# Linear attention and a mixture of experts on one core: key values turned by VectorE and a way over DRAM, in place of TensorE transposes

## The reference

```
xn  = layernorm(x)                                  # rows of 128
# linear attention, H = 16 heads of DK = 8, F = 64 features a head
q, k, v = xn @ Wq + bq, xn @ Wk + bk, xn @ Wv + bv   # split into heads
qp = relu(q @ rw) + EPS;  kp = relu(k @ rw) + EPS    # per head: 8 -> 64
kv   = sum over the 256 rows of kp^T v               # per batch and head, 64 x 8
out  = (qp @ kv) / (qp @ kp.sum(rows) + EPS);  attn = out @ Wo + bo
# experts, E = 8, 128 -> 512 -> 128, one expert a row
gate = p1 / (p1 + p2) of softmax(xn @ wr + br);  e = argmax
ffn  = gate * (gelu(xn @ w1[e] + b1[e]) @ w2[e] + b2[e])
result = x + attn + ffn
```

## Time and profile before

| what | value |
|---|---|
| profiled execution | 205.19 us, its span 203.2 us |
| median of 3 runs | 205.25 us (204.72 to 205.96) |
| PE busy | 189.6 us, 93% |
| DVE, ACT, POOL busy | 66%, 65%, 60% |
| granted TensorE clock, mean | 0.988 |
| DMA | 29.48 MB, 145 GB/s over the span |

### The profile page before, as it was taken

One profiled execution on the slowest core, in us unless ns is written; L12 is line 12 of the kernel. 1 busy time (PEld: TensorE's weight loads), 2 busy tenths in 40 slices (PEclk: granted clock), 3 DMA queues, 4 the chain that ended last, 5 costly groups with the idle time before them and its releaser, 6 DMA issues. The chain is left out here.

```text
span 203.2 us, 6913 instructions
## 1 busy us (share of the span) xinstructions
PE 189.6 (93%) x2353; PEld 151.1 (74%) x2353; DVE 134.9 (66%) x467; ACT 133.0 (65%) x319; POOL 121.0 (60%) x156
## 2 busy tenths in 40 slices
PE   6799999898899999999999999999999999999960
PEld 6557676565566666666666668999999999999950
DVE  5899697668888877777777786555555545545540
ACT  3268868659977777777777754755655655655620
POOL 2059793101137666666666210788888888888884
PEclk9999999999999999999999999999999999999995
DMA  4730599999912221222267293899999999996330
GB/s 140 220 102 14 150 210 185 111 266 304 243 34 68 68 68 65 68 70 68 67 175 250 56 261 93 216 182 183 194 213 210 220 204 198 214 220 129 28 33 3
DMA packets 32464, 29.48 MB, mean 145 GB/s; under 512 B 5904, under 2 KB 24752, under 8 KB 32432
## 3 DMA queue, kind: packets, MB, share of 16 engines
q1 hardware_dynamic: 25792, 24.82, 49.2%
q0 software_dynamic: 6640, 4.24, 14.9%
HBM read 20.10 MB, written 11.49 MB: 155 GB/s over the span
## 5 line engine op out<-in xcount | busy, mean ns | idle before, releaser
L452 POOL DMA_INDIRECT out<-k_all,slots_all x39 | 60.9, 1562 | 21.8 <-DMA out<-res 9.6
L823 ACT ACTIVATE q_all<-feat,w_slot 128x128 f32<-128x128 f32 x156 | 44.5, 369 | 29.1 <-PE feat L671 29.1
L422 POOL DMA_INDIRECT sorted_x<-rows_all,place_i x32 | 31.5, 984 | 16.6 <-PE feat L556 9.7
L671 PE MATMUL feat<-v_all,w_slot 128*128 128x128 f32 x312 | 41.3, 275 | 0.0
L671 PEld LDWEIGHTS feat<-v_all,w_slot 128*128 128x128 f32 x312 | 38.0, 192 | 0.4 <-issue 0.4
L417 POOL TENSOR_SCALAR o_bias<-kv_sum,den_eps 128x1 f32<-128x1 f32 x32 | 8.6, 270 | 29.0 <-PE feat L543 22.8
L683 PE MATMUL o_bank<-w_sb,q_all 128*128 x160 | 21.2, 276 | 0.2 <-ACT q_all L823 0.2
L1090 DVE SCALAR_TENSOR_TENSOR gated_b<-b_all,slots_all,out_row 128x128 f32<-128x128 f32 x39 | 13.7, 352 | 11.1 <-issue 11.1
L770 ACT ACTIVATE k_feat<-feat 128x512 f32<-128x512 f32 x16 | 9.6, 597 | 16.4 <-PE feat L543 16.2
L683 PE MATMUL feat<-w_sb,q_all 128*128 x152 | 20.1, 275 | 0.0
L683 PEld LDWEIGHTS o_bank<-w_sb,q_all 128*128 128x128 f32 x160 | 19.4, 192 | 0.4 <-issue 0.4
(11 more groups left out here) (142 smaller groups left out, 322.3 us busy)
## 6 DMA issues: line engine op xcount, KB each, us to landing
w_slot<-w1x SPq DMA_DIRECT2D x39, 258.0 KB, 3.7
sorted_x<-ones_f SPq DMA_DIRECT2D x1, 2535.0 KB, 22.1
w1x<-in_w SPq DMA_DIRECT2D x1, 2048.0 KB, 26.5
out<-res SPq DMA_DIRECT2D x16, 128.0 KB, 2.3
x_all<-in_x SPq DMA_DIRECT2D x7, 256.0 KB, 5.8
slots_all<-sorted_x SPq DMA_DIRECT2D x23, 65.0 KB, 3.9
out<-k_all,slots_all POOLq DMA_INDIRECT x39, 4.8
slots_all<-sorted_x SPq DMA_DIRECT2D x1, 520.0 KB, 4.9
```

Of the source, the lines that this page charges most:

```text
L422: pool.indirect_dma_start(sorted_x, bass.IndirectOffsetOnAxis(ap=place_i[:, t:t + 1], axis=0), rows_all[:, t, :], None).then_inc(x_moved, 16)
L452: pool.indirect_dma_start(out_rows, bass.IndirectOffsetOnAxis(ap=slot_rows[j % SLOT_RING][:, D + 1:XW].bitcast(I32), axis=0), y_sb[j % Y_R ...
L671: ins = pe.matmul(bank[:, a * P:(a + 1) * P], w1_slot[j % W1_RING][:, a * P:(a + 1) * P], xsT[j % X_RING][:, :], start=True, stop=True)
L823: act.activation(hidden_T[j % H_RING][:, a * P:(a + 1) * P], hid_bank[j % HID][:, a * P:(a + 1) * P], ACT.Gelu, bias=w1_slot[j % W1_RING][ ...
```

## The change

The key values of batches 0 to 13 are no longer turned by PE. DVE transposes `kv_T` in blocks of 32x32 into `kv_turn`; SP writes that to a DRAM buffer (128 KB), waits until it has landed, and reads it back into `ka` in four DMAs (32 partitions each, runs of 256 bytes), so that the blocks change places. Batches 14 and 15 are still turned by PE, in the tail. Queries run one iteration behind keys and outputs three (before: none and two). The rotation over three `feat` tensors begins in iteration 0; ranks, the transposed b1 and the late projections go to `o_bank`'s bank. On SP the residual stores and the first six w1 loads stand between the batches' ways over DRAM, and the other w1 loads wait for the landing of the last store. The diff, cut to its core:

More of the change, by code:

```diff
@@ L230, in build @@
         b2_gated = sem("b2_gated")
+        kv_turned = sem("kv_turned")
+        kv_out, ka_in = [sem(f"kv_out{n}") for n in range(2)], [sem(f"ka_in{n}") for n in range(2)]
         y_ps, y_ready = sem("y_ps"), sem("y_ready")
@@ L532, in k_features @@
             def k_features(b):
[L533 to L538 removed]
+                if b == 1:
+                    pe.wait_ge(k_act, 1)
+                    pe.wait_ge(k_dve, 1)
+                elif b > 1:
+                    pe.wait_ge(k_act, 2 * b)
+                    pe.wait_ge(q_act, 2 * b - 3)
+                    pe.wait_ge(q_dve, b - 1)
+                banks = key_pair(b)
                 for k in range(K):
@@ L547, in q_features @@
             def q_features(b):
-                pe.wait_ge(k_act, 2 * b + 2 if b < TURNING else 2 * b + 1)
-                pe.wait_ge(k_dve, b + 1)
-                due(pe, q_act, 2 * b)
-                pair = feat_pair(2 * b + 1)
+                if b < NBATCH - 1:
+                    pe.wait_ge(k_act, 2 * b + 3)
+                    pe.wait_ge(k_dve, b + 2)
+                    due(pe, q_act, 2 * b)
+                else:
+                    pe.wait_ge(k_act, 2 * b + 2)
+                    pe.wait_ge(q_act, 2 * b - 1)
+                    pe.wait_ge(q_dve, b)
+                banks = query_pair(b)
                 for half in range(2):
@@ L574, in key_values, with turn_last @@
                 ins.then_inc(kv_ps, 1)
-            def turn(i):
-                due(pe, ka_ready, i - 1)
-                pe.wait_ge(kv_ready, 2 * i)
-                for par in range(2):
-                    ins = pe.transpose(turned_bank(i)[:, par * P:(par + 1) * P], kv_T[(i - 1) % 2][:, par, :], ident[:, :])
+            def turn_last():
+                pe.wait_ge(kv_ready, 2 * NBATCH)
+                pe.wait_ge(q_act, 2 * (NBATCH - 1))
+                for b in range(TURNED, NBATCH):
+                    for par in range(2):
+                        at = (b - TURNED) * S + par * P
+                        ins = pe.transpose(kt_bank[:, at:at + P], kv_T[b % 2][:, par, :], ident[:, :])
                 ins.then_inc(turn_ps, 1)
@@ L660, in turn_slot @@
                 rows_in(pe, j)
+                if j == 0:
+                    pe.wait_ge(q_dve, NBATCH)
                 if j >= 2:
@@ L1046, in _ @@
             dve.wait_ge(mask_ready, 8)
-            for i in range(NBATCH):
+            k_relu(0)
+            for i in range(1, NBATCH):
+                if 2 < i <= TURNED:
+                    turn_kv(i - 1)
                 k_relu(i)
-                if i == 0:
+                if i == 1:
                     find_top(CHUNKS // 2 - 1)
+                    mask_kv(0)
+                    turn_kv(0)
+                if i == 2:
+                    scan_rows()
+                    list_earlier()
+                if i == 3:
+                    count_slots()
+                    rows_of_slots()
+                if i >= 4:
+                    scale_tokens(i - 4)
+                if i == 4:
+                    place_rows()
+                if i == 6:
+                    name_experts()
+                if i >= 4:
+                    turn_tokens(i - 3)
+                q_relu(i - 1)
                 if i == 1:
                     pick(CHUNKS // 2 - 1)
-                    scan_rows()
+                if i == 2:
+                    read_ranks()
+                if i == 3:
+                    pick_rows()
+                    turn_tokens(0)
+                if i >= 4:
+                    residual(i - 4)
                 if i >= 3:
-                    scale_tokens(i - 3)
-                if i == 2:
-                    count_slots()
-                    find_first()
+                    invert_sums(i - 3)
                 if i == 3:
-                    read_ranks()
-                    place_rows()
-                if i == 4:
                     place_gates()
@@ L1102, in _ @@
             dve.wait_ge(b2_in, 16)
+            scale_tokens(12)
+            q_relu(15)
+            q_relu_last()
+            turn_tokens(13)
+            invert_sums(13)
+            residual(12)
             scale_tokens(13)
```

182 lines of the change are left out of this document (87 added, 95 removed).

## The result

The changed kernel takes 228.45 us (median of 4 runs, 228.01 to 229.2) against 205.01 for the kernel before in the same measurement (4 runs): ratio 1.1122, 95% interval 1.109 to 1.1154. The forecast was 220.4, with a range up to 227; the time lies 8 us above the one and 1.5 above the other. The profiled execution took 228.15, its span 226.4, so 23.2 us more than before.

A forecast was written before the change was run, and what follows sets the result against it. The prediction took PE's own work to bound the loop, each microsecond removed being worth its length. Its terms, 10.5 + 2.1 - 4.8 + 1.6 + 4.3 + 1.5, gave +15.2, so 220.4 us, range 211 to 227.

The forecast's parts named there:

- The start, +10.5: Outputs in iteration 3 wait for batch 0's key values over DRAM, starting at 61.6 instead of 51.12: +10.5 us.
- The rival of the write that passes the fills: Batch 0's write lands at 56.1, ahead of the large loads, outputs start at 59.7: 218.5 us, chance 0.08.
- The bound below, 8.6: Low bound of the late start: write lands 2.1 us after issue at 54.0, outputs start at 59.7, +8.6 us.
- Removed turns and DVE's transpose, -4.8 and +1.6: Loop: 12 turns off PE save 0.40 us each, -4.8; DVE's new transpose delays k_relu, +1.6; period 4.79 us.
- Work behind the start, +2.1: The one-iteration shift leaves one more outputs step and one more q_features step behind the late start: +2.1 us.
- SP's pace, +4.3: w1 loads in iterations 8 to 13 stretch SP's period to 5.85 us, so PE waits for key values: +4.3 us.
- My upper bound of 6.7 for the period, with the term at 9: High case for SP in the w1 iterations: write late by 1 us, 0.48 a read; period 6.7, term 9 us.
- The clock, +1.5: After the long wait in iteration 3 PE restarts at half clock: +1.5 us, bounds 0 and 4.
- dearer in each iteration: Rival: slow 256-byte runs or held-up reads make SP's period 5.2, then 6.7 us: 226 to 229 us, chance 0.12.

The follow-up runs named there:

- b1_late: Changed kernel with the copy of b1 moved behind batch 0's write and reads in SP's list; 229.77 us, ratio 1.052 to the kernel before (chip A).
- w1_behind2: Changed kernel with the first six w1 loads moved behind the batch loop; 220.74 us on chip B, where the kernel before takes 205.6.
- pe_turn: Changed kernel with all key values turned by PE and nothing over DRAM; 218.58 us, ratio 1.0019 (chip C); run again on chip B, 205.95 us, ratio 1.0015.
- b1_late2: Changed kernel with the copy of b1 behind batch 0's way over DRAM, run again on chip D; 231.49 us, ratio 1.0531 to the kernel before.
- turn_off2: Kernel before without PE's transposes of key values in the loop, result left wrong; 219.08 us, ratio 0.9981 (chip D).

## Why the prediction was right and wrong

*The start, +10.5: right in kind, measured +7.7.* `outputs` in iteration 3 waited for a DMA into `ka`, after a write that landed just behind the large loads and four reads. From the first read's issue to `outputs` were 3.2 us, 3.5 forecast. The rest is the landing: w2, issued at 32.76 instead of 34.23, landed after 22.0 us (23.2 in the earlier trace rows), at 54.8, and the write by 55.6; I had 58.0, from one execution of before. The rival of the write that passes the fills did not happen. The bound below, 8.6, was too high, since it let SP be held for 7.46 us where it was 4.97: that figure of the earlier trace rows is not a property of the copy, which in b1_late, behind the first reads, held SP for 0.43 us.

*Removed turns and DVE's transpose, -4.8 and +1.6: the step that failed.* I took "PE 4.99 of 5.00" as proof that each microsecond taken out is worth its length. It was worth nothing: iterations 4 to 12 took 0.8 us more than before, not 2.2 less (eight times 5.06 - 4.79). Full occupancy and a ring of equal length look alike in busy time. The evidence was in the earlier trace rows and in the row of `pk` beside them: `out_project` can't start before ACT's `pk`, which stands behind relus that wait for this iteration's key features. I followed DVE's chain from masking to k_relu and never ACT's from key features to `pk`. DVE's transpose, 0.45 us as forecast, did no harm: DVE waits 0.77 us for `pk` behind it.

*Work behind the start, +2.1: right in kind, measured +3.2.* In w1_behind2, which has no other waits there, the stretch from the last key features to `outputs(14)` is 8.46 us (120.38 to 128.84) against 5.25, so +3.2, for `outputs(13)`, q_features and the late transposes and `out_project` that moved ahead of it.

*SP's pace, +4.3: mechanism right, size wrong.* SP does fall behind in the iterations with a w1 load and only there. Its turn took 7.13 us in place of 5.85: from write to first read 3.3 (2.65 forecast), the reads 2.1 (1.84), from the last read over store and w1 load to the next write 1.7 (1.36), each as a mean of the five turns. None is wrong by much, and together they double the term: w1_behind2 puts all that the w1 loads cost by `outputs(14)` at 11.3 us. About 2.8 of them are clock (next point), 8.5 pace. My upper bound of 6.7 for the period, with the term at 9, was too low for the period.

*The clock, +1.5.* The first restart cost what the row says, 1.94, 2.09 and 1.46 where the same steps take 1.07, 1.15 and 1.09: +2.2. Of it 0.7 is left at the next key features, since before, a wait of 0.52 us, the transposes and `out_project` stood in this iteration too. Not foreseen: behind the waits of 2.65 and 2.80 us PE restarts at half clock too, another 0.9 + 0.5 and 0.9 + 0.6 us. I had priced the clock at one place and SP's waits without it.

*The rivals.* What happened lies nearest to "dearer in each iteration", 226 to 229 with a chance of 0.12, though for another reason: the ways over DRAM without a w1 load beside them keep pace. The time came out above the range because two terms erred the same way, by 4.0 (turns) and by 7.0 with the clock (SP), and the start erred by only 2.8 the other way. I had let the range take such errors one at a time.

By the measured terms: 7.7 + 0.7 + 0.8 + 3.2 + 11.3 = 23.7 against 23.4 on the marks; the overlap of 0.3 is not resolved. The rule of the Trainium skill, "DMA: Bandwidth & Descriptors", section "Issuing engines are not separate DMA queues", that initiating a DMA is usually small beside the DMA, does not fit these small DMAs: four reads hold SP 1.76 us of the 3.2 from their first issue to PE's start, and behind the large loads one issue held it 12.34 us.

No version here beats the kernel before; pe_turn equals it at 205.95.

## What to carry to other kernels

Before taking work out of an engine that looks full, follow for one iteration each dependence from its first instruction, over the other engines, back to it: if that ring is as long as the iteration, the work is worth nothing until the ring is shortened too, and what is next to it must be known as well. When a step goes into a queue that serves a loop, add up the queue's whole turn with a wait's full price, its landing and the clock that PE loses behind it, and keep large loads that have time out of that turn. The first small transfer behind large ones pays for them, in whichever order the small ones stand.

## What the runs showed of the hardware

*An issue behind large loads that have not landed holds its engine.* The same 128 KB writes mostly took SP 0.34 to 0.43 us once the fills of `sorted_x` and w1x and the load of w2 had landed, and 1.76 (changed kernel), 12.34 (b1_late) and 12.88 us (b1_late2) behind them. SP was free again at 51.4 to 53.9 in all the kernels that write batch 0 this way, however early the issue began. That it waits for room in the queue is my reading; no trace shows the queue's filling.

*Among four equal reads one is sometimes slow.* Mostly the four hold SP for 1.73 to 1.79 us, in some iterations for 2.1 to 3.5 (the slowest single one for 2.0, in w1_behind2), with and without a w1 load ahead. What decides it wasn't tried.

*The half clock can follow a short wait.* At 122.02 and 135.48 PE restarts at half clock after idling 2.65 and 2.80 us; at 109.50, after 3.03 us, it does not (1.07). The table by stages of the changed kernel shows the return (columns of the earlier trace rows):

```profile
62.00:64.00 2.00, 2.00 (x40) 1.20 (x36) 1.04 (x3) 1.14 (x2) 0.00 (x0) 0.62 0.23 71
64.00:66.00 2.00, 2.00 (x40) 1.14 (x32) 1.90 (x9) 1.05 (x3) 0.00 (x0) 1.00 0.25 58
```

From the restart at 58.84 the clock is at 0.50 (1.2 GHz) until within 62 to 64 and at 1.00 (2.4 GHz) from 64 on.

*Chips differ.* The same kernel before takes 205.0 us in the first measurement and 205.6 on chip B, and 218.3 to 219.6 on chips A, C and D. There PE's key features, 1.15 us in the one case, have gaps in each iteration from the sixth or so on, at a mean granted clock of 0.996, as in this row of turn_off2:

```profile
79.52 2.30 PE L543 MATMUL feat<-rw_bd,k_all 32*128 32x256 f32 x16
```

The engine waits for nothing that the trace shows. GpSimd's moves of rows begin at about the same time, but the run meant to part the two came onto the other kind of chip. The cause stays open.
